# Making a graph layer's keys at the head of the scores pass instead of in the table stage

## What is computed

```
h = layernorm(x)                                     # [3125, 256], rows of m.x, columns in m.xT
q, k, v = h @ Wq.T + bq, h @ Wk.T + bk, h @ Wv.T + bv
e = sum over a head of q[src] * k[dst] / sqrt(64)    # one score per edge and head
m = segment_max(e, dst);  ex = exp(e - m[dst])
rst = segment_sum(ex / segment_sum(ex)[dst] * v[src], dst)
```

## Time and profile before

| | us |
|---|---|
| median of 3 runs | 3035.8 |
| lowest and highest | 3034.43 and 3038.24 |
| span of the profiled execution | 3034.9 |
| PE busy in it (88%), DVE (67%), ACT (46%), POOL (35%) | 2658.5, 2046.7, 1386.4, 1056.6 |
| first stage, to the last v out of PSUM | 95.7 |
| first instruction of the scores pass (SP) | 99.31 |
| first and last multiply of the pass | 110.93 and 628.43 |

### The profile page before, as it was taken

The page is one execution under the profiler, slowest core; times in us unless marked ns, Lnnn a source line. Parts: engine busy times, 40 slices in busy tenths (PEclk is TensorE's granted clock), DMA queues, the critical chain, the costliest instruction groups (busy, mean ns, idle before and its releaser), DMA issues. The chain is left out here.

```text
span 3034.9 us, 54933 instructions
## 1 busy us (share of the span) xinstructions
PE 2658.5 (88%) x12024; PEld 2082.7 (69%) x12025; DVE 2046.7 (67%) x4093; ACT 1386.4 (46%) x2925; POOL 1056.6 (35%) x1184
## 2 busy tenths in 40 slices
PE   8777787778994999999989999999979977869698
PEld 6545565465553777777767888888858865647587
DVE  6676777868888553644226888888889958955411
ACT  2214332228882343343323444444389948845122
POOL 1576777732111000000006666666500008810033
PEclk9897899999996999999999999999979989989799
DMA  4699999927774000000017777777601131042353
GB/s 134 221 317 290 294 309 302 320 84 227 228 225 131 21 1 9 9 1 10 9 38 241 213 214 215 214 216 212 189 17 36 53 125 60 1 177 87 98 172 129
DMA packets 236592, 443.80 MB, mean 146 GB/s; under 512 B 29017, under 2 KB 128801, under 8 KB 235068
## 3 DMA queue, kind: packets, MB, share of 16 engines
q1 hardware_dynamic: 179518, 261.89, 27.8%
q0 software_dynamic: 56960, 180.47, 18.8%
HBM read 350.56 MB, written 92.69 MB: 146 GB/s over the span
## 5 line engine op out<-in xcount | busy, mean ns | idle before, releaser
L1889 PE MATMUL bank<-sums 128*128 128x256 f32 x2352 | 543.0, 381 | 2.6 <-issue 2.6
L1965 POOL DMA_INDIRECT conv_h<-table_h,conv_ix x392 | 373.9, 954 | 293.7 <-ACT conv_ix L1936 172.1
L1889 PEld LDWEIGHTS bank<-sums 128*128 128x128 f32 x2352 | 435.6, 191 | 54.6 <-issue 3.0
L1696 ACT ACTIVATE area<-bank,nodes_bi,nodes_sc 128x320 f32<-128x320 f32 x320 | 197.5, 617 | 350.6 <-PE bank L1604 350.6
L714 POOL DMA_INDIRECT x<-table_qv,scores_ix x300 | 286.7, 956 | 186.9 <-ACT scores_ix L618 109.1
L1867 DVE SCALAR_TENSOR_TENSOR x<-bank,nodes_w,x 128x256 f32<-128x256 f32 x200 | 96.4, 484 | 300.1 <-PE bank L1613 300.0
L1424 PE MATMUL bank<-attend_pv,x 128*128 128x260 f32 x800 | 220.6, 405 | 26.8 <-POOL attend_pv L1354 24.6
L734 PE MATMUL bank<-sums,area 128*128 x800 | 232.2, 419 | 10.7 <-issue 6.2
L1424 PEld LDWEIGHTS bank<-attend_pv,x 128*128 128x128 f32 x800 | 137.9, 191 | 109.2 <-issue 62.6
L1936 ACT ACTIVATE conv_ix<-src 128x2 int32 x196 | 39.9, 203 | 359.8 <-DVE conv_msg L1986 346.8
L1986 DVE TENSOR_TENSOR conv_msg<-bank,conv_h 128x512 f32<-128x512 f32 x196 | 135.6, 692 | 91.2 <-PE bank L1889 81.6
(11 more groups left out here) (488 smaller groups left out, 5763.2 us busy)
## 6 DMA issues: line engine op xcount, KB each, us to landing
sums<-in_edges SPq DMA_DIRECT2D x196, 384.0 KB
x<-edge_v SPq DMA_DIRECT2D x200, 256.0 KB, 3.0
edge_v<-x SPq DMA_DIRECT2D x150, 256.0 KB
hidden_rows<-top_wide SPq DMA_DIRECT2D x25, 512.0 KB, 3.4
projected<-spline_hst SPq DMA_DIRECT2D x10, 960.0 KB, 4.4
ball_hT<-projected SPq DMA_DIRECT2D x5, 1920.0 KB, 17.3
top_wd<-in_top_wd SPq DMA_DIRECT2D x8, 1024.0 KB
x<-in_x SPq DMA_DIRECT2D x10, 640.0 KB, 9.1
```

The source lines that it names most:

```text
L1696: nc.scalar.activation((h1, h2)[layer][:, o, hf * CW:(hf + 1) * CW], banks[n % HIDS][:, 0:CW], ACT.Relu, scale=sc[:, layer, e, o:o + 1], b ...
L1889: mm = nc.tensor.matmul(banks[u][:, g * F:(g + 1) * F], m.conv_eT[:, u, g, c], m.conv_w[:, c], start=False, stop=c == EC - 1, skip_group_c ...
L1965: nc.gpsimd.indirect_dma_start(out=h[:, u, g, :], out_offset=None, in_=m.d_h, in_offset=bass.IndirectOffsetOnAxis(ap=ix[:, u * G + g:u * G ...
```

## The change

The first stage makes q and v only. The keys' weights and bias are loaded last among its loads, into SBUF that the mixing layer's weight `wqT` and its context take later (`m.key_w` is `wqT`, `m.key_b` the second half of `mix_both`). At the head of the scores pass PE makes the keys of all 25 tiles, in a ring of six banks, between its second and third `spread_out`; DVE adds the bias after its first two `one_hot`; ACT makes the half-window copies tile by tile, 2 x 24 of 64x256, in place of the two large copies. PE begins with `keys` when all is added and copied. The load of `wqT` waits on SP until all keys are made, ahead of the first store of v.

```diff
-    KINDS = 3
+    KINDS = 2
...
-                for j, n in enumerate("qkv"):
+                for j, n in enumerate("qv"):
...
+                sp.dma_start(m.key_w, a["gnn_wk"]).then_inc(keys_loaded, 16)
+                sp.dma_start(m.key_b, a["gnn_bk"]).then_inc(keys_loaded, 16)
                 for t in range(NT):
-                    sp.wait_ge(biased, 2 * t + 1)
+                    sp.wait_ge(biased, t + 1)
...
                 def products(t):
                     pe.wait_ge(copied, t + 1)
-                    for j in range(2):
-                        i = 2 * t + j
-                        if i >= 3:
-                            pe.wait_ge(biased, i - 2)
-                        for f in range(FT):
-                            mm = nc.tensor.matmul(bank(i), m.xT[:, f, t * P:(t + 1) * P], w[:, j, f], start=f == 0, stop=f == FT - 1)
-                        mm.then_inc(product, 1)
+                    if t >= 3:
+                        pe.wait_ge(biased, t - 2)
+                    for f in range(FT):
+                        mm = nc.tensor.matmul(bank(t), m.xT[:, f, t * P:(t + 1) * P], w[:, 0, f], start=f == 0, stop=f == FT - 1)
+                    mm.then_inc(product, 1)
...
-                    nc.vector.tensor_tensor(qv[:, t % U, 0:F], bank(2 * t), b[:, 0], ALU.add).then_inc(biased, 1)
-                    dve.wait_ge(product, 2 * t + 2)
-                    nc.vector.tensor_tensor(keys[:, t], bank(2 * t + 1), b[:, 1], ALU.add).then_inc(biased, 1)
+                    nc.vector.tensor_tensor(qv[:, t % U, 0:F], bank(t), b[:, 0], ALU.add).then_inc(biased, 1)
...
+        KEY_BANKS = (6, 7, 0, 1, 2, 3)
...
+                sp.wait_ge(key_made, NT)
+                sp.dma_start(m.wqT[:], a["mix_wqT"]).then_inc(mivec_loaded, 16)
                 rounds = rounds_of(sp, m, RING)
...
-                nc.scalar.activation(k[0:P // 2, NT:SLOTS], k[0:P // 2, 1:NT], ACT.Copy).then_inc(k_spread, 1)
+                for t in range(1, NT):
+                    act.wait_ge(key_kept, t + 1)
+                    nc.scalar.activation(k[0:P // 2, NT + t - 1], k[0:P // 2, t], ACT.Copy).then_inc(k_spread, 1)
+                    nc.scalar.activation(k[P // 2:P, NT + t - 1], k[P // 2:P, t - 1], ACT.Copy).then_inc(k_spread, 1)
...
+                for u in range(UN - 2):
                     spread_out(0, u, pe.snap(carried[u]))
-                pe.wait_ge(k_spread, 2)
+                for t in range(NT):
+                    if t >= len(KEY_BANKS):
+                        pe.wait_ge(key_kept, t - len(KEY_BANKS) + 1)
+                    for f in range(FT):
+                        mm = nc.tensor.matmul(key_bank(t), m.xT[:, f, t * P:(t + 1) * P], m.key_w[:, f], start=f == 0, stop=f == FT - 1)
+                    mm.then_inc(key_made, 1)
+                spread_out(0, UN - 2, pe.snap(carried[UN - 2]))
+                pe.wait_ge(key_kept, NT)
+                pe.wait_ge(k_spread, 2 * (NT - 1))
...
-                c_(nc.vector.memset(m.context[:], 0.0))
...
-                nc.vector.tensor_copy(k[P // 2:P, NT:SLOTS], k[P // 2:P, 0:NT - 1]).then_inc(k_spread, 1)
...
+                for t in range(NT):
+                    dve.wait_ge(key_made, t + 1)
+                    nc.vector.tensor_tensor(k[:, t], key_bank(t), m.key_b, ALU.add).then_inc(key_kept, 1)
+                dve.wait_ge(key_kept, NT)
+                c_(nc.vector.memset(m.context[:], 0.0))
```

## The result

| | before | changed |
|---|---|---|
| median (16 runs each) | 3035.63 us | 3027.32 us |
| lowest and highest | 3031.5, 3038.47 | 3018.11, 3038.19 |
| profiled execution: span | 3034.9 | 3016.4 |

The ratio is 0.9976, with an interval from 0.9968 to 0.9985: 7.3 us faster, between 4.6 and 9.7, and 8.3 by the medians. I had said 13.5 faster. The sign is right, and the time lies in the range, but the gain by the medians is only three fifths of what was said. Its stages can.

The account below looks back on a forecast made before the run. Bounds: PE in the steady first stage, DVE before tile 9, step 40's multiply in the scores pass. Stage gains 13.8 + 9.4 + 2.7 + 0.6 = 26.5 us, less 13.0 late, is 13.5: 3022.3 us median, range 3012 to 3031.

Parts of the forecast that it names:

- First stage, steady part: Tiles 9 to 24 of the first stage: 1.945 us a tile instead of 2.81, gaining 13.8 us.
- First stage, before tile 9: From tile 0's bias to the second comparison's end, DVE sheds key adds and idle time: 9.4 us, 7.4 if PE runs cold.
- POOL's term: Early first stage: a long POOL instruction holding a small DVE one starts its chain sooner; 0.6 us, between 0 and 1.2.
- List to tile 9: First stage, from the second comparison's end to tile 9's products: 2.3 us remain of 5.0, gaining 2.7, or 0.8.
- The keys on PE: Head of the scores pass: 25 tiles of keys, 5.2 us at half clock, then 19.0 at full clock.
- The copies on ACT: Head of the scores pass: two copies per tile stay under PE's 0.865 us; only the last tile's show, 1.3 with the add.
- The first multiply: Scores pass, in the clock of before: the first multiply comes at 128.8 instead of 110.93, 17.9 us late.
- POOL's stall: Scores pass, before step 8: POOL's gather comes at about 130.2 instead of 123.70, a stall of 6.5 us.
- Catching up: Scores pass to step 39: late multiplies run at 2.36 us a step, leaving the pass 13.0 us late at its turning point.
- the rival without catching up: Scores pass: DMA queues hold the multiplies 17.9 us late; 8.6 us gained, 3027.2 us; chance 0.2.
- the one in which the cover swallows more: Rounds 5 to 9 run at POOL's pace, so only its 6.5 us stall counts; 20.0 us gained, 3015.8; chance 0.15.
- a first stage that keeps its length before tile 9: First stage before tile 9 doesn't shrink: 13.8 us gained and 13.0 given back, 3035.0 us; chance 0.1.

Follow-up runs that it names:

- unread matmuls: Changed kernel plus 21 matmuls whose results nobody reads, in PE's gaps: 3024.77 us; the same with the lower-half copies on DVE: 3029.13 us.
- The halves taken alone: Kernel before with only the new first stage, keys zeroed: 3015.26 us; with only the new head, keys made twice: 3054.57 us.
- the four variants that reach step 199 before 617 us: New first stage with old pass, 3015.26 us; changed kernel with half key sums and shared copies, 3027.45; with PE gaps filled, 3024.77; that with shared copies, 3029.13.

## Why the prediction was right or wrong, step by step

- **What bounds the kernel: right.** POOL's pace at the end of the pass, the multiplies in rounds 5 to 9, and so step 40 as the turning point. Steps 40 to 80 took 119.35 us against 119.28, and POOL still waited 14.7 us where it had waited 14.4.
- **First stage, steady part: right in size per tile, wrong in reach.** 1.95 us a tile, but tiles 9 and 10 ran at 1.2 GHz, (3.84 - 1.95) + (2.63 - 1.95) = 2.6 us, so the sixteen tiles gave 11.2 and not 13.8. This is the largest term that was mis-sized: I had counted all sixteen at the clock of the earlier trace rows. In the two further profiles tiles 9 and 10 cost 1.7 and 2.6 us in the same way. The faster PE has itself made a gap here. Before, PE was still making tile 8 when the comparison ended; now it had been idle for 1.5 us. That the gap, with the small matmuls behind it, is what cost the clock fits all six profiles without unread matmuls, but one of the two with them ran cold too.
- **First stage, before tile 9: the mechanism right, the size 1.8 too large.** DVE's chain got 8.2 us shorter, where 9.4 + 0.6 were said. From the bias of tile 0 on it got 8.0 shorter. What is missing of the 9.4 is about what DVE waits for a cold PE at tiles 3 and 4, 1.6 us. I had named that case, at 7.4, and not taken it. POOL's term gave 0.2 instead of 0.6 (20.65 for 20.87). POOL's three instructions come 0.64 us earlier, and its long one no longer holds L131 for 2.22 us; but the two ahead of it now hold L392 and L394, normally of 0.16 us, until they end themselves:

```profile
14.39 1.14 POOL L263 CAST sums<-sums 128x1152 f32<-128x1152 int32 x1 [7.12 <-DMA sums<-in_dst_lines]
14.51 1.03 DVE L392 SCALAR_TENSOR_TENSOR front_slot<-front_tile,front_slot 99x2 f32<-99x2 f32 x1
...
15.59 1.16 POOL L265 CAST lines<-sums 128x1152 bf16<-128x1152 f32 x1
15.77 0.99 DVE L394 SCALAR_TENSOR_TENSOR front_sums<-front_slot,front_count 99x1 f32<-99x1 f32 x1
...
19.46 0.24 DVE L131 TENSOR_SCALAR front_mean_var<-front_mean_var 128x5 f32<-128x5 f32 x1
```

  In the two further profiles of the same program the meeting went worse: three such instructions took 1.06, 0.98 and 2.23 us, and 1.13, 0.98 and 2.23. There tile 0's bias starts at 22.5, later than before the change, and the comparison ends only 4.9 and 6.3 us earlier than in the first profile of before. So even the sign of this term changes between executions, and its bounds of 0 and 1.2 were too narrow.

- **List to tile 9: right**, 2.4 us for 2.7.
- **The sum of the stage: 21.8 instead of 26.5**, just below the lower bound of 22.0; in the two further profiles 19.7 and 19.9. The bounds lacked a term for the clock behind the list, and one for a worse meeting of POOL and DVE.
- **The keys on PE: right**, 24.47 us for 24.2, with 1.2 GHz up to 86.3 and full clock behind it, and no wait for a bank.
- **The copies on ACT: right only in that they nearly hid.** At 0.42 us each they ended 1.65 us behind PE (1.3 said). That they need as long as PE, and so bar any gain from faster keys, I had not seen: "two of them stay under PE's 0.865" was wrong by a hair.
- **The first multiply: 1.7 us later than said.** In the clock of before (the pass began 21.7 us earlier) it is at 130.5, not 128.8: 0.6 from PE, 0.35 from ACT, and 0.74 from the way to the multiply.
- **POOL's stall: 11.3 us instead of 6.5** (11.57 with its usual 0.30 between gathers), and without effect, as said. 2.6 of it are the copy that no longer holds the second gather (0.96 us where it was 3.54), the rest mostly the later multiply. The rule of the Trainium skill, "SBUF — State Buffer" (the part with the trap "DVE blocks DMA" and the one above it), agrees with the rows at both places: without the large copy the second gather is short, and beside the 25 adds the gathers still take 0.95 us, one every 1.25.
- **Catching up: right.** Step 0 to step 8 took 18.91 us (18.9 said), step 39 came at 221.1 in the clock of before (220.9 said), and step 40 was 13.3 us late (13.0 said). That step 39 is hit to 0.2 us is in part luck: the first multiply was 1.7 us late, and the 39 steps took 90.6 us instead of 92.1. But from the last v to step 40 all three profiles of the changed kernel need 13.3 to 14.3 us more than the kernel before (131.2, 132.1 and 131.1 for 117.8). The 98% busy DMA engines did not hold the multiplies, so the rival without catching up is out. So is the one in which the cover swallows more: rounds 5 to 9 had a clock of 0.79 instead of 0.76, and took as long. The two rivals that lose, a first stage that keeps its length before tile 9 and keys made wholly at 1.2 GHz, are out by the 8.2 and 24.47 us.
- **The net.** -21.8 + 13.3 = -8.5 us at step 40, where the trace shows -8.4, and the medians differ by 8.3. The head's term, which I thought the less certain, was right to 0.3 us; the error of 5 us is that of the first stage: 2.6 + 1.4 us of clock, 0.4 of POOL's holding of DVE, and 0.3 behind the list. Over all three profiles step 40 gains 7.1 us, and there POOL's part is larger.
- **What stays open.** The halves taken alone give -18.5 and +22 us by the timed runs, which would add up to a loss, while at the last multiply they give -23.2 and 12.5 to 17.1, which adds up to the measured gain. A scatter of some 9 us behind the pass also appears in the kernel before, but it may not be all: the four variants that reach step 199 before 617 us need 2408.1 to 2411.9 us from there, where the two kernels took 2397.1 to 2406.6 and the one that makes the keys twice 2404.7 to 2408.6. With one profile of each, whether an earlier end of the pass is partly lost behind it is not settled. The mean clock from 620 to 3016 us is 0.95 in all five profiles of the two kernels and doesn't tell them apart.

## What to carry over

When a change takes work from the engine that sets the pace, look for the places where this engine will now wait for another one, and price them twice: the wait, and a clock that may be low behind it. Ask also which instructions of two engines will now meet that did not meet before. Work that is moved beside other work ends with the slowest of its helpers: sum every engine's share per tile, with the row of exactly that shape, before one is called hidden. And read a gain of 0.3% at the end of the stage that was changed, in more than one profile, since what lies behind it may scatter by more, and the stage itself by 2 us.

## What the runs showed of the hardware that was not expected

- 78 matmuls of 99x1 keep PE "busy" without a gap in the records, and yet the granted clock fell to 0.51 while they ran and for 6.8 us in all, behind only 1.5 us of idleness. In all six profiles without unread matmuls tile 9 was cold at least in part. Before, the same 78 matmuls, directly behind full ones, left the clock at 1.00, and so did 2.19 us of idleness with full matmuls behind it. With three unread matmuls of 128x256 ahead of the 78, one profile stayed at 1.00 and one did not (0.84 from 35 to 46 us).
- Small DVE instructions of 0.16 us lasted until a POOL instruction that had started just before them ended: 1.03, 0.99 and, in the kernel before, 2.22 us, beside POOL's 1.14, 1.16 and 2.36. Which of them meet differs between executions of one program, and moves its first stage by 2 us.
- An ACT copy of 64x256 within SBUF takes 0.42 us, as much as a full 128x256 add on DVE, while one of 64x6144 takes 5.30: 24 small ones cost 10.6 us instead of 5.3. The same small copy on DVE takes 0.29.
- The same program scatters by 9 us behind the scores pass (2397.1 and 2406.5 us for the kernel before). Rounds 5 to 9 scatter less: they took 119.4, 121.1 and 118.1 us in three profiles of the changed kernel.
